# One register for the bound of 768 indirect scatters, loaded ahead of the loop

## What is computed

```python
h = tok_ref(x, W, b, token, pos)            # 14 x 14 patches, one matmul each: 197 rows with the class token
h = concatenate([h, txt], axis=1)           # 128 text rows behind them: 325
h = h + attn_ref(layernorm(h), ...)         # a phase memory in place of softmax attention
h = h + ffn_ref(layernorm(h), ...)          # the change lies in the routing of this one

def ffn_ref(x, gate_w, w1, w3, w2, sw1, sw3, sw2):
    scores = sigmoid(xf @ gate_w.T)                       # 64 experts
    top_scores, top_idx = top_k(scores, 2)                # two experts a row
    pos = cumsum(one_hot(flat_e), axis=0)[...] - 1        # place of the row in its expert
    buf = zeros((64, 256, d)).at[flat_e, pos].set(x_pairs, mode='drop')   # 256 places, later rows are dropped
    y = (silu(buf @ w1) * (buf @ w3)) @ w2
    routed = weighted sum of each row's two results
    shared = (silu(xf @ sw1) * (xf @ sw3)) @ sw2
    return shared + routed
```

## Time and profile before

| | us |
|---|---|
| median of 3 runs | 1799.02 |
| lowest and highest run | 1791.42, 1825.51 |
| span of the profiled execution | 1823.6 |

### The profile page before, as it was taken

The page is one execution under the profiler, slowest core; times in us unless marked ns, Lnnn a source line. Parts: engine busy times, 40 slices in busy tenths (PEclk is TensorE's granted clock), DMA queues, the critical chain, the costliest instruction groups (busy, mean ns, idle before and its releaser), DMA issues.

```text
span 1823.6 us, 30829 instructions
## 1 busy us (share of the span) xinstructions
PE 1534.0 (84%) x9237; PEld 1158.6 (64%) x9237; DVE 1421.6 (78%) x5705; ACT 1256.5 (69%) x2195; POOL 1226.0 (67%) x973
## 2 busy tenths in 40 slices
PE   2888998999899999888989898999889975676672
PEld 1566776777676767656767666677667764554552
DVE  3477997999797988777888888889888975587661
ACT  2897997988788878777878787889878851111110
POOL 1025776777676767666667676777667767488887
PEclk9899999999999999999999999999999998899886
DMA  9965666666666666556555655566656221476653
GB/s 182 229 138 120 138 139 125 123 121 124 102 117 100 117 101 106 96 103 103 95 101 104 108 102 102 101 111 105 103 103 103 63 59 40 96 116 109 98 88 35
DMA packets 267117, 197.21 MB, mean 108 GB/s; under 512 B 65464, under 2 KB 246437, under 8 KB 266953
## 3 DMA queue, kind: packets, MB, share of 16 engines
q1 hardware_dynamic: 210120, 174.84, 50.2%
q0 software_dynamic: 51200, 17.87, 8.4%
q10 hardware_dynamic: 5633, 2.56, 0.7%
HBM read 86.24 MB, written 85.39 MB: 94 GB/s over the span
## 4 chain that ended last, share of the span: by engine, by line
PE 40%; ACT 22%; issue 11%; POOL 9%; another core or an unknown queue 8%; DVE 7%; DMA 3%; SPq 0%; ACTq 0%; POOLq 0%; DVEq 0%
POOL out_rows L639 6%; PE bank L919 5%; PE bank L999 5%; ACT img L656 5%; ACT xh L739 4%; PE bank L1087 3%; PE bank L982 3%; POOL slot_rows L605 3%; PE bank L946 2%; PE bank L1018 2%; PE bank L1078 2%; ACT xs L726 2%; ACT kq L793 2%; ACT kq L792 2%
## 5 line engine op out<-in xcount | busy, mean ns | idle before, releaser
L605 POOL DMA_INDIRECT slot_rows<-xs,slot x768 | 874.1, 1138 | 284.5 <-issue 247.3
L656 ACT ACTIVATE img<-img 84x980 f32<-84x980 f32 x190 | 339.6, 1788 | 14.8 <-DMA img<-in_x 7.2
L591 POOL TENSOR_TENSOR rs<-ve,neg_half 128x12 f32<-128x12 f32 (+1 forms) x66 | 150.3, 2277 | 234.4 <-DVE ve L1342 232.8
L919 PE MATMUL bank<-img,w_tok 126*128 126x392 f32 (+1 forms) x640 | 228.7, 505 | 27.9 <-DMA img<-img 23.3
L639 POOL DMA_INDIRECT out_rows<-img,etok x128 | 198.7, 1552 | 64.0 <-issue 35.0
L919 PEld LDWEIGHTS bank<-img,w_tok 126*128 126x128 f32 (+1 forms) x640 | 124.0, 195 | 113.3 <-issue 23.3
L982 PEld LDWEIGHTS bank<-pos_a,v 128*128 128x128 f32 x768 | 145.4, 198 | 54.0 <-issue 10.8
L982 PE MATMUL bank<-pos_a,v 128*128 128x325 f32 (+2 forms) x768 | 163.8, 351 | 6.1 <-issue 3.8
L726 ACT ACTIVATE xs<-h,nb,rs 128x128 f32<-128x128 f32 x384 | 154.0, 481 | 3.0 <-DVE nb L1348 3.0
L739 ACT ACTIVATE xh<-h,nb,rs 128x128 f32<-128x128 f32 x384 | 154.0, 480 | 1.3 <-DVE nb L1348 1.3
L1499 DVE TENSOR_TENSOR h<-bank,hbo 128x768 f32<-128x768 f32 x64 | 61.1, 955 | 114.6 <-remote 103.3
(11 more groups left out here) (217 smaller groups left out, 3697.1 us busy)
## 6 DMA issues: line engine op xcount, KB each, us to landing
img<-in_x SPq DMA_DIRECT2D x384, 150.1 KB
img<-img SPq DMA_DIRECT2D x254, 160.8 KB
img<-img SPq DMA_DIRECT2D x128, 128.6 KB
out_rows<-fin SPq DMA_DIRECT2D x128, 128.0 KB
slot_rows<-xs,slot POOLq DMA_INDIRECT x768
slot_rows<-init_rows SPq DMA_DIRECT2D x16, 540.0 KB, 9.1
img<-slot_rows SPq DMA_DIRECT2D x32, 270.0 KB
h<-in_txt SPq DMA_DIRECT2D x64, 128.0 KB
```

The source lines that it names most:

```text
L591: g.tensor_tensor(out=rs[:, q.u, half:], in0=ve[:, q.u, half:], in1=neg_half[:, half:], op=ALU.pow).then_inc(S["p_rs"], 1)
L605: g.indirect_dma_start(out=slots_d, out_offset=bass.IndirectOffsetOnAxis(ap=slot[0:nt, q.x, r, part:part + 1], axis=0), in_=xs[0:nt, q.x, ...
L656: a.activation(cols[:, b0:b0 + nb, :], raw[:, q.u, :].rearrange("p (t b) -> p b t", b=P)[:, b0:b0 + nb, :], ACT.Copy)\
L919: ins = mm(bank[:, 5, 0:2 * PATCHES], w_tok[r, m, :], xk[r, k.u, :, m, :], start=(m == 0), stop=(m == SHIFT - 1))
```

## The change

The bound of the check was given as a number, and the language made of it a register load ahead of each of the 768 scatters. Now one register is loaded ahead of the loop and named in each scatter. The order of all else stays. As the wait for v_slot stood on the first register load of a pair, it now stands on the first scatter itself.

```diff
             pool.wait_ge(s_pre_p, 3)
 
+            last_slot = pool.to_reg(SLOTS - 1)
+
             def rstd(q):
...
                     g.indirect_dma_start(
                         out=slots_d, out_offset=bass.IndirectOffsetOnAxis(
                             ap=slot[0:nt, q.x, r, part:part + 1], axis=0),
-                        in_=xs[0:nt, q.x, part, :], in_offset=None, bounds_check=SLOTS - 1,
+                        in_=xs[0:nt, q.x, part, :], in_offset=None, bounds_check=last_slot,
                         oob_is_err=False).then_inc(s_scat[q.x], 16)
```

## The result

| | before | changed | ratio, 95% interval |
|---|---|---|---|
| the chip of the case | 1799.74 us | 1890.80 us | 1.050 (1.043 to 1.057) |
| chip 13 | 1789.88 us | 1906.23 us | 1.069 (1.046 to 1.092) |
| chip 11 | 1662.45 us | 1661.98 us | 0.9993 (0.998 to 1.0006) |

The forecast was 1797.5 us, no change. It failed on the first line and held on the third. I call them late and punctual chips, by what the traces show of PE. Medians are of all runs; a ratio leaves out the slow ones, those over 1.5% above the fastest of the same kernel.

What follows compares the result with a forecast made beforehand. PE and ACT were taken to set the pair loop's pace, some 22 us a pair, with POOL a side branch. Terms summed to 0 to -4.5 us, taken as -1.5: 1799.02 - 1.5 = 1797.5 us, range 1784 to 1812.

Steps and rivals of the forecast that it cites:

- POOL's own terms: Effects on POOL's queue, its waits, nb and the loop's end: 0 to -4.5 us in sum, taken as -1.5.
- nothing between two scatters: Register loads between scatters (22.3 us of POOL's sequencer) are hidden behind descriptor work; the distance stays 0.30 us, no gain.
- 0.36 to 0.50 us once a pair: Ahead of a pair's first scatter, the load behind the v_slot wait goes: 21 us less idle time on POOL together.
- the hidden stall: Second scatter 0.47 us late in 14 pairs, every 48 scatters; taken as hidden afterwards, 6.9 us of POOL's idle time.
- 1.5 us at nb: DVE's nb waits for POOL's rs; two such waits, 0.58 and 0.91 us, would go.
- no gain at the end: After the loop POOL is done 0.5 to 1 us earlier, but the expert-row fetch has over ten us of cover: nothing.
- 24.6 us: Stated distance over the median of the run nearest the profiled one, when putting the same 1.5 us to the median.
- where the 21 to 28 us of POOL's idle time go: POOL would wait longer for DVE's ve instead; only nb's waits for rs could gain, 1.5 us, at most 4.5.
- The rival on PE's pauses: Scatters shifted by 0.4 us move packets against transfers feeding PE; runs scatter -8 to +26 us anyway; 11%, either sign.
- The rival of DVE standing still: Earlier first scatters straddle other DVE instructions and hold DVE up: 31 to 62 us slower, 1830 to 1861 us; 3%.

Runs made afterwards that it cites:

- change_c: The changed kernel unaltered, run again as a control on chip 13, a late one: 1.069 of the kernel before.
- mult_before_c: The changed kernel plus one small POOL multiplication (128x6) between the v_slot wait and each pair's first scatter: 1.020 on late chip 13; as mult_before, 1.001 on punctual chip 4.
- bound_zero_e: The changed kernel with 0 in the shared register instead of 16383, so almost no row is written: 1.061 of the kernel before on chip 14, late.
- load_first: The changed kernel, but each pair's first scatter loads its own bound; the other eleven share the register: 0.9999 on chip 4, 0.9946 on late chip 13.
- six_before: The changed kernel plus six small POOL multiplications (128x1) between the v_slot wait and each pair's first scatter: 1777.67 us, 0.9641 of the kernel before, chip 14, late.

## Why the prediction was wrong

*POOL's own terms* were right, one by one: nothing between two scatters, 0.36 to 0.50 us once a pair, the hidden stall, 1.5 us at nb, no gain at the end. A reader can rely on this working, and on a punctual chip its sum agrees with the result, 1662.45 to 1661.98 us, though 1.5 us is too little to be told there. One number in it is off and nothing hangs on it: 24.6 us is what the profiled span has over the median; the run of 1825.51 us has 26.5.

*The step that failed* is the one on where the 21 to 28 us of POOL's idle time go: "It is worth something only where POOL was late for rs and nb waited for it." It counts what POOL can do to others through semaphores, and in that way POOL costs nothing. In its place the runs showed DVE waiting for late results of PE, 160.2 us in place of 103.3 at h, 32.1 us more idle time of PE and 25.5 us more of busy time at a lower granted clock. The term that was most wrong is the stall of every 48th scatter, of which the forecast said that "both ends come to nearly the same in the end": the 12 pairs that lost it are 3.7 us longer each. Runs with the same wait structure (change_c and mult_before_c differ in one multiplication of 0.23 us that nobody waits for) differ by some 5%. What passes from POOL to PE here is no semaphore but the moment at which POOL's scatters run.

*The rival on PE's pauses* had the right place, the 103.3 us of the earlier trace rows, and had the shift as its cause on record ("a shift of 0.4 us in the scatters moves their packets against those of the transfers that feed PE"), but was written off as noise: "no effect of the change but can look like one", 11%, either sign. Three runs between 1791 and 1826 were taken for a measure of it. A wait that is 103 us long, that no instruction explains and that sits in the time in which the change moves something, isn't noise of the run; it is larger than every term of the sum. To price it, nearest at hand were the 14 pairs of the earlier trace rows, whose second scatter comes 0.47 us late: in the trace of before twelve of them take 20.6 us on the average and the pairs with the usual distance 23.3. With the stall hidden, as I forecast, these pairs become like the others: 12 x 2.7 = 32 us, over half of the 57.6 us between the traces and a third of the 91 between the medians. The prediction used the gap and not the periods.

*The rival of DVE standing still* came to the right side, with a smaller size (1830 to 1861, measured 1890.8), by a mechanism that the runs exclude: L1476 stays at 948 ns.

*Packets.* The recorded cause speaks of packets. Bytes of the scatters it isn't (bound_zero_e). Whether it is the packets' number, POOL's descriptor work, or the semaphore steps that they end in is open. In favour of the last, argued and not shown: in the changed kernel's trace 71% of PE's late records lie within 0.05 us of a DMA's step of some semaphore, and 31% of the same moments moved 1 us later do. But of PE's records that come on time 52% do as well, so this weighs little. Kernels that take away most of the spreads and the stores met only punctual chips, so their part is open as well. So is what makes a chip late.

## What to carry to other kernels

Read the time of the unchanged kernel beside every experiment first: here its 1664 us in place of 1800 told that the effect belongs to a kind of chip. Where a profile shows an engine's results coming later than its records, price everything that the change moves in that stretch by pairs of the trace that already have the other timing, even if no semaphore joins them. And a register that saves loads behind a wait may better be loaded once more at the head of each group: load_first has one load in place of twelve and takes 0.9999 of the time before on a punctual chip and 0.9946 (0.989 to 0.9999) on a late one. It loses nothing, and its gain is within what these runs can hardly tell. six_before is faster on a late chip (0.964), but wasn't run on a punctual one, where the smaller delay of mult_before came to 1.001, no difference clear of the noise. And a long pause of the engine that sets the pace should be priced with what follows it: here the granted clock fell behind such pauses.

## What the hardware showed that was not expected

- One program takes 1662 to 1664 us on chips 3, 4, 7 and 11 and 1790 to 1845 us on chips 13 and 14 and on that of the case. Chip 14 was late both times; every other chip was met once, so whether a chip keeps its kind isn't shown. PE's finished steps come up to 5 us late and more on the second kind, mostly in one part of the loop, and nearly all of them at the full clock: 296 of the 302 late ones of the kernel before.
- The granted clock of the profiled run is 0.965 for the changed kernel on chip 11, 0.956 for the kernel before on the chip of the case and 0.942 for the changed one there (0.936 to 0.944 in the three other runs with a start of 0.42 us). From 300 to 1300 us the trace of chip 11 has no stretch at 1.2 GHz.
- A delay of the first scatter by 0.1 us (0.42 to 0.52) is worth some 5% on such a chip (1.069 - 1.020; the two intervals leave 1 to 9%). One by 1.4 us is worth 10% by the ratios of two groups (1.06 to 0.964) and 7% by their times (1905.85 to 1777.67 us, both on chip 14).
- The traces of late chips also hold fewer semaphore records: of the 12288 steps of the scatters' four semaphores, 4758 before and 12064 on chip 11. The missing ones may hide some lateness or feign it in my counts; the waits in the profile's own rows don't hang on the counts.
- Whether the recording has a part in the lateness can't be told from runs that are all recorded, and no run here shows it. The Trainium skill, in NOTIFIC — the notification-queue block, section 7.1 Overflow: three behaviours, one of which stalls the engine, has a full ring either drop records or hold up the producer, and the block's inner pipeline always hold up rather than lose. Lost records and late steps side by side would fit both halves of it; that only PE is late is not explained by it.
- With an instruction's wait on the indirect DMA itself, the first scatter of a group follows the one before it at 0.30 us, over the group's boundary; a register load that carries the wait makes 0.65 us of it.
